# A selective-scan layer with routed experts: round-off, carries and residual move to other engines, the first chunk's front gets five PSUM banks, and the orders are planned anew

## The reference, cut to what matters

```python
x = x + mamba(layernorm(x))          # then
x = x + moe(layernorm(x))

# mamba(x):
xn = layernorm(x) * ln_g + ln_b
u, z = split(xn @ W_in.T)            # 512 + 512 features
u = silu(causal_conv4(u) + conv_b)
dt, B, C = split(u @ W_xp.T, [16, 32])
dt = softplus(dt @ W_dt.T + b_dt)    # 512 features
h = exp(dt * A) * h + (dt * u) * B   # per token, 512 features x 16 states
y = (h * C).sum(states) + u * D
return x + (y * silu(z)) @ W_out.T

# moe(x): the best 2 of 8 experts per token, weights by softmax of their logits
return sum_k w_k * (silu(x @ gate[e_k]) * (x @ up[e_k])) @ down[e_k]
```

## Time and profile before

| | us |
|---|---|
| median of 3 runs | 2536.23 (2534.64 to 2537.91) |
| profiled execution | 2529.41 |
| its span, first to last instruction | 2527.6 |
| first scan, end of the last unit (from the span's start) | 111.25, 2349.4 |
| mean granted TensorE clock | 0.848 |

### The profile page before, as it was taken

How to read it: one execution, slowest core, us unless ns; L and a number is a source line. 1 busy time by engine, 2 the same in 40 slices (tenths; PEclk the granted TensorE clock), 3 DMA queues, 4 the chain that set the end, 5 groups by cost and what they waited for, 6 DMA issues and landing times.

```text
span 2527.6 us, 31861 instructions
## 1 busy us (share of the span) xinstructions
PE 1826.6 (72%) x7502; PEld 912.5 (36%) x7502; DVE 2152.9 (85%) x3108; ACT 1629.0 (64%) x2921; POOL 1901.5 (75%) x1220
## 2 busy tenths in 40 slices
PE   5566757586878778686877678687877768665775
PEld 1112313143434344342434334343434434343543
DVE  0299999999998999899999999999999999999411
ACT  3667666667677677676767676666767667754232
POOL 0478786888878797987878797878978788888333
PEclk9877868697988888797989888798978879887898
DMA  1445444465847576575847666675757656688332
GB/s 51 118 101 117 97 113 110 104 177 147 196 126 191 138 185 159 155 178 129 205 125 188 145 164 161 155 183 135 197 135 186 155 144 163 156 225 234 101 60 35
DMA packets 217976, 369.30 MB, mean 146 GB/s; under 512 B 31040, under 2 KB 86592, under 8 KB 217664
## 3 DMA queue, kind: packets, MB, share of 16 engines
q1 hardware_dynamic: 192208, 333.56, 51.5%
q0 software_dynamic: 25584, 33.71, 6.8%
HBM read 285.05 MB, written 83.01 MB: 146 GB/s over the span
## 4 chain that ended last, share of the span: by engine, by line
PE 29%; issue 23%; DVE 19%; POOL 14%; ACT 10%; DMA 4%; POOLq 0%; DVEq 0%; ACTq 0%; SPq 0%
DVE dA L1030 10%; PE ring L568 7%; POOL arena L1260 4%; DMA out<-yt,xt 4%; PE yps L654 4%; PE ring L559 3%; ACT dA L900 3%; POOL sorted_x L1294 3%; PE ring L574 3%; DVE arena L1030 3%; PE p_g L686 3%; POOL arena L1268 2%; PE p_a L666 2%; PE ring L585 2%; POOL rst L1232 2%
## 5 line engine op out<-in xcount | busy, mean ns | idle before, releaser
L1260 POOL TENSOR_TENSOR arena<-arena,b_bc 128x2048 f32<-128x2048 f32 x256 | 1023.4, 3998 | 30.9 <-PE yps L654 30.8
L900 ACT ACTIVATE dA<-arena,a_s 128x512 f32<-128x512 f32 x1024 | 673.7, 681 | 316.9 <-DVE arena L1041 220.5
L1030 DVE TENSOR_TENSOR_SCAN dA<-dA,carry,arena 128x512 f32<-128x512 f32 x384 | 477.3, 1273 | 27.3 <-ACT dA L900 27.3
L1030 DVE TENSOR_TENSOR_SCAN dA<-dA,arena 128x512 f32<-128x512 f32 x384 | 454.0, 1213 | 42.2 <-ACT dA L900 41.6
L654 PE MATMUL yps<-arena,const_s 128*32 128x512 f32 x2048 | 328.3, 717 | 220.9 <-POOL arena L1268 179.2
L1268 POOL TENSOR_TENSOR arena<-arena,c_bc 128x511 f32<-128x511 f32 (+1 forms) x256 | 323.7, 1264 | 193.2 <-DVE arena L1030 189.7
L559 PE MATMUL ring<-arena 128*128 128x512 f32 x512 | 300.4, 717 | 198.3 <-ACT sz L825 126.0
L1304 POOL DMA_INDIRECT out<-yt,xt x135 | 218.2, 1616 | 137.4 <-DMA out<-yt,xt 67.7
L1041 DVE TENSOR_TENSOR arena<-dA,c_bc 128x1024 f32<-128x1024 f32 x256 | 312.3, 1220 | 4.4
L568 PE MATMUL ring<-arena 128*128 128x512 f32 x512 | 266.4, 668 | 21.3 <-ACT xn_t L887 9.6
L1060 DVE SCALAR_TENSOR_TENSOR t_s<-t_s,arena 128x512 f32<-128x512 f32 x64 | 158.6, 2477 | 95.5 <-ACT t_s L843 95.5
(11 more groups left out here) (147 smaller groups left out, 2870.5 us busy)
## 6 DMA issues: line engine op xcount, KB each, us to landing
arena<-dt_d SPq DMA_DIRECT2D x512, 256.0 KB, 5.6
w_e<-in_w_moe SPq DMA_DIRECT2D x105, 512.0 KB, 4.6
dt_d<-arena SPq DMA_DIRECT2D x128, 256.0 KB, 2.6
w_e<-in_w_moe SPq DMA_DIRECT2D x105, 256.0 KB, 4.4
xt<-sorted_x SPq DMA_DIRECT2D x135, 129.0 KB, 5.2
b_bc<-bc_d SPq DMA_DIRECT2D x256, 64.0 KB, 2.7
c_bc<-bc_d SPq DMA_DIRECT2D x256, 64.0 KB, 2.2
xs<-in_x SPq DMA_DIRECT2D x16, 512.0 KB, 8.6
```

The lines of the kernel that those rows point to most:

```text
L900: act.activation(dA[:, j, :], rep_dt[:, c % 2, j, :], ACT.Exp, scale=a_s[:, n, j:j + 1]).then_inc(s_exp, 1)
L1030: return dve.tensor_tensor_scan(out_ap, dA[:, j, :], hs[:, u % 3, j, :], init, ALU.mult, ALU.add)
L1260: pool.tensor_tensor(hs[:, u % 3], rep_dtu[:, c % 2], b_bc[:, g, :].unsqueeze(1).to_broadcast([P, J, T]), ALU.mult).then_inc(s_dbu, 1)
```

## The change

- **Round-off to GpSimd.** ScalarE makes t = 1 - (1 + e) in one more Identity; GpSimd adds e (`round_off`); `less_lost` now adds.
- **Carries to ScalarE.** `keep01` and `keep2` copy the last columns, each after VectorE's product; the next unit's exponentials wait for the copy.
- **Residual to TensorE.** `out_proj` adds the identity times `xs` in PSUM; ScalarE evicts the sum to `xs` (kind O in `take`). All items of the ring are now evicted by ScalarE.
- **Five banks.** The first 16 items of chunk 0 (X, U, W, P, Z, D0) go in turn to `ring` and the four banks of `dA`, before the scans need these; chunk 0 has tables of its own (`MAKES0`, `TAKES0`). The diagonal matrices of the convolution are made in four parts, VectorE's `tables` come later, and chunk 1's statistics come before all else in the front.
- **Orders.** Tables, places in the loop bodies and tile slots are new: a scatter per slot for 8 slots in place of two for 4, the last batch's tiles at +19 for +17.

```diff
-TILE_AT = [18, 20, 22, 24, 26, 28, 29, 31]
-TAIL_AT = 17
+TILE_AT = [17, 20, 22, 24, 26, 28, 29, 31]
+TAIL_AT = 19
...
-        a_slot = 2 if q >= NQ - 2 else 2
+        a_slot = 2 if q >= NQ - 2 else 1
...
-            self.at = [self.ready + k for k in [20, 21, 22, 23, 24, 25, 27, 28]]
+            self.at = [self.ready + k for k in [18, 20, 21, 22, 23, 25, 26, 28]]
...
-         (17, 0): ["O0"], (18, 0): ["O1"], (19, 3): ["F0"], (20, 1): ["F1"], (21, 4): ["R0"], (23, 4): ["K0"]}
...
+MAKES0 = {(-20, 1): ["X0", "X1"], (-19, 1): ["U0", "U1"], (-18, 1): ["W0", "U2"], (-17, 1): ["W1", "U3"], (-16, 1):
...
+FIVE = sum(q == 0 and name[0] in "XUWPZ" or name == "D0" and q == 0 for q, name in RING)
+BANK = {item: k % 5 if k < FIVE else 0 for k, item in enumerate(RING)}
+BEFORE = {}
+for k, item in enumerate(RING):
+    BEFORE[item] = next((o for o in reversed(RING[max(0, k - 5):k]) if BANK[o] == BANK[item]), None)
...
+        def bank(q, name):
+            k = BANK[q, name]
+            return dA[:, k - 1, :] if k > 0 else ring[:, :]
...
             def out_proj(q, a):
                 pe.wait_ge(s_yg, CC * (q + 1))
+                pe.wait_ge(s_xs, q + 1)
                 for i in range(2 * a, 2 * a + 2):
                     for c in range(CC):
-                        last = pe.matmul(ring[:, i % 2 * DM:i % 2 * DM + DM], sz[:, q % 2, c, i * P:(i + 1) * P],
-                                         w_out_s[:, c, :], start=c == 0, stop=c == CC - 1)
+                        pe.matmul(ring[:, i % 2 * DM:i % 2 * DM + DM], sz[:, q % 2, c, i * P:(i + 1) * P],
+                                  w_out_s[:, c, :], start=c == 0, stop=False)
+                    last = pe.matmul(ring[:, i % 2 * DM:i % 2 * DM + DM], ident, xs[:, q % 3, i, :], start=False, stop=True)
...
             def make(item):
-                k = MADE[item] - 2
-                if k >= 0:
-                    pe.wait_ge(s_ract if evictor(RING[k]) == "act" else s_rdve, TAKEN[RING[k]])
+                last = BEFORE[item]
+                if last:
+                    pe.wait_ge(s_ract, TAKEN[last])
...
             for s in range(FIRST, TOTAL_SLOTS):
+                for item in made_in(s, 0):
+                    make(item)
                 if 0 < s <= UN * NQ:
                     weigh(s - 1)
-                for item in made_in(s, 0):
-                    make(item)
...
-                act.activation(t_s[:], dtub[:, c % 2, :], ACT.Identity, bias=1.0).then_inc(s_s, 1)
+                act.activation(t_s[:], dtub[:, c % 2, :], ACT.Identity, bias=1.0).then_inc(s_one, 1)
+                act.wait_ge(s_one, v + 1)
+                act.activation(t_s[:], t_s[:], ACT.Identity, bias=1.0, scale=-1.0).then_inc(s_s, 1)
...
+                if kind == "O":
+                    act.activation(xs[:, q % 3, 2 * c:2 * c + 2, :], ring[:, :].rearrange("p (i d) -> p i d", d=DM), ACT.Copy).then_inc(s_ract, 1)
...
                 wait(act, s_m01 if j < 2 else s_m2 if j == 2 else s_h3, u)
+                if u > 0 and (u - 1) // UN % 2 == 0 and j != 3:
+                    act.wait_ge(s_carry01 if j < 2 else s_carry2, UN * ((u - 1) // UN // 2) + (u - 1) % UN + 1)
                 act.activation(dA[:, j, :], rep_dt[:, c % 2, j, :], ACT.Exp, scale=a_s[:, n, j:j + 1]).then_inc(s_exp, 1)
+            def keep01(u):
+                act.wait_ge(s_m01, u + 1)
+                act.activation(carry[:, u % UN, 0:2], dA[:, 0:2, T - 1], ACT.Copy).then_inc(s_carry01, 1)
...
-                if q % 2 == 0:
-                    dve.tensor_copy(carry[:, n, 0:2], dA[:, 0:2, T - 1]).then_inc(s_carry, 1)
...
-            def round_off(q, c):
-                dve.wait_ge(s_s, CC * q + c + 1)
-                dve.scalar_tensor_tensor(t_s[:], t_s[:], 1.0, dtub[:, c % 2, :], ALU.subtract, ALU.subtract).then_inc(s_t, 1)
...
-                dve.tensor_tensor(dst, ring[:, :].rearrange("p (i d) -> p i d", d=DM), dst, ALU.add).then_inc(s_rdve, 1)
...
+            def round_off(q, c):
+                pool.wait_ge(s_s, CC * q + c + 1)
+                pool.tensor_tensor(t_s[:], t_s[:], dtub[:, c % 2, :], ALU.add).then_inc(s_t, 1)
...
-                for c, at in enumerate((-8, -3, 0, 4)):
-                    if (s - at) % UN == 0 and 0 <= (s - at) // UN < NQ:
-                        less_lost((s - at) // UN, c)
+                for p, k in pieces(s, (-8, -2, 0, 3), (-11, -1, 1, 3)):
+                    less_lost(p, k)
...
+                for p, k in pieces(s, (-9, -3, -1, 2), (-12, -3, 0, 2)):
+                    round_off(p, k)
```

More of the change, by code:

```diff
@@ L298, in mamba_moe @@
         s_s = sem("s_s")
+        s_one = sem("s_one")
         s_l = sem("s_l")
@@ L506, in _ @@
                 front = 0 <= q + 1 < NQ
+                for g, k in tiles_in(s + 1):
+                    load_tile(g, k)
+                if q >= 0 and front and n == 9 or s == -13:
+                    store_bc(q + 1)
+                for g, k in tiles_in(s - 1, False):
+                    load_down(g, k)
                 if n == 4 and 0 <= q - 1 < NQ:
@@ L966, in _ @@
                         second_weight(p)
+                for item in taken_in(s, 0):
+                    take(item)
+                for p in ahead(s, 12, -9):
+                    norm_x(p)
                 if 0 <= s + 1 < UN * NQ:
@@ L1195, in _ @@
                     unit_second(s)
+                if n == 7 and tail:
+                    route(q - 1)
+                if unit:
+                    unit_last(s)
+                if tail and n == 2:
+                    moments(1, q - 1)
+                for p in ahead(s, 10, -21):
+                    moments(0, p)
                 if unit and n in (4, 8, 12):
```

206 lines of the change are left out of this document (97 added, 109 removed), and 24 rows, old and new, of tables (MAKES, MAKES0, TAKES, TAKES0).

## The result

The changed kernel takes 2393.45 us in the median of 4 runs (2382.61 to 2405.61) against 2536.72 us: ratio 0.9437, 95% interval 0.9391 to 0.9484, some 143 us less. The forecast was 2354 us, range 2280 to 2430. The profiled execution took 2390.97 us, its span is 2389.1.

The account below looks back on a forecast made before the run. VectorE was taken to bound the unit window (2110.94 of 2238.15 us). Front 95 + window 2075 (work 1923 + idle 152) + tail 175 = 2345 us of span, 2354 us against the median of runs; range 2280 to 2430.

Parts of the forecast that it names:

- Front, 95: Stretch before the first scan: first scan at 95 us, 16 us gained, within bounds of 6 and 25.
- VectorE's work, 2111 - 188 = 1923: Unit window: round-off 152, carries 18 and residual 18 us leave VectorE, so its work falls to 1923 us.
- reordering inside a slot adds nothing: Slots of the unit window: moving gated product, statistics and routing behind the last product adds nothing to VectorE's work.
- All of it on the engine that sets the window.: Unit window: all 188 us come off VectorE, whose work has hardly a gap that could swallow them.
- Idle, 127 + 25 = 152: VectorE's idle time in the unit window: new waits, chiefly late drive products, add 1.6 us a chunk, 25 us.
- as long as nobody waits for that item: Output projection on TensorE: the residual's extra matmuls, 30 us in all, are free on that condition.
- rival 2: Unit window: the replan removes waits, VectorE's idle halves to 64 us, time 2266 us; chance 0.13.
- Carries: Copies moved to ScalarE: 18 us off VectorE, the delay to exponentials covered; cost 0, upper end 51 us.
- Tail, 175: Stretch after the last scan: one addition earlier gives -4.6 us, two output projections cost +1.9, so 175 us.
- Rival 1: Unit window: GpSimd and TensorE become the bound, the full 100 us of new idle, 2429 us; chance 0.17.
- Rival 4: TensorE's unit reduction behind ring items in six of 16 slots delays scans; 2594 us at 2.5 us a slot; chance 0.04.
- Rival 3: VectorE beside GpSimd: other instructions wait for GpSimd's longer queue, returning 115 us, time 2469 us; chance 0.05.

Follow-up runs that it names:

- the square: Four kernels with and without the change's two halves: neither 2532 us, three moves only 2527.49, new order and five banks only 2410.98, both 2393.45.
- the moves alone: Kernel before with round-off to GpSimd, carries to ScalarE and residual to TensorE, in the old order and old front: 2527.49 us, ratio 0.9979.
- the order and banks alone: Changed kernel's tables, places and five banks, with round-off, residual and carry copies on VectorE again: 2410.98 us, ratio 0.9535.
- the one-bank run: Changed kernel with the first chunk's items all in one bank, new tables kept: 2423.07 us, ratio 0.9563.

## Why the prediction was right, and where it was not

The time came out 39 us above the forecast and inside its range; the totals of the stretches were near. That is in good part luck. The sum credits the moves with 188 us and the order within the slots with nothing, while in the square the moves alone bring 5 us and the order and banks alone 118; the errors cancelled. The signs named for being right (the first scan, VectorE's work and idle time, GpSimd 88% busy) all came near, and none of them could tell the two apart.

- **Front, 95.** Measured 87.2. The banks were credited 6 us (seven gaps of 0.84 us) and the order the rest; the one-bank run shows all but 2 us depend on the banks. In the two traces the four U items and the four convolutions take TensorE from 17.87 to 50.5 us with one bank and from 16.29 to 39.1 with five, so by the projection P the difference is 11 us (54.6 and 43.2). The other 11 arise behind it, where ScalarE waits 9.2 us for the Z items with one bank and not at all with five. The prediction counted the gaps before TensorE's items, not the waits of ScalarE behind them.
- **VectorE's work, 2111 - 188 = 1923.** Measured 1949. The 188 us were read rightly as what the three groups cost: 168 went in the old order. But "reordering inside a slot adds nothing" failed in both directions. The new order alone takes 65 us off VectorE, 60 of them from the round-off's stretch, which the sum had booked to its move. And it adds some back: before the change an independent instruction stood between a scan and its product in many places, which now follow each other directly. From the records, scan to product is 1.24 us start to start and scan to an independent instruction 1.115; some 138 more pairs are adjacent, 17 us. Putting `activate` between gave 11 us of work back and no time.
- **"All of it on the engine that sets the window."** This is the step that failed. VectorE's 94% of the window in the earlier trace rows was taken for the bound of every slot. The moves in the old order took 168 us off it and won 3 us of window. Under the new order 96 us off won 20.
- **Idle, 127 + 25 = 152.** Measured 178; the size was near, the source not as told. The drive's lateness was foreseen and costed at 25 us; it measures 57.6. The wait of the statistics for the evicted output projection was missed: TensorE's extra matmuls were called free "as long as nobody waits for that item", and the statistics did, 37.6 us in the window (the residual's own wait for TensorE, 38.0 with the order alone, went). That the replan takes idle time away (25 us) stood only in rival 2.
- **Carries.** "VectorE has 3 us before it needs those exponentials, and that covers it": alone they cost 21 us instead of gaining 18; the round-off got longer (13) and so did the wait for the exponentials (18).
- **Tail, 175.** Measured 174.5; the order alone has 175.0. The split (-4.6, +1.9) was not tested.
- **Rival 1** (GpSimd as bound, 2429) was partly at work: 21 of 55 us taken off GpSimd came out of the window. **Rival 2** had the replan's sign right. **Rival 4** (TensorE late with `weigh`) did not reach VectorE: the gated product waits 5.9 us for it, 32.4 before. GpSimd's drive does wait longer for TensorE, 63.7 us for 30.8, but with the order alone that wait is 72.1 us, and the scans wait only 5.5 us for the drive there.
- **Rival 3** (the stretch changes owner) came true in the small. No 128x512 instruction and no scan got longer; but routing's small ones, which have two operands in SBUF, now stand beside GpSimd's product. After, and before:

```profile
L1131 DVE TENSOR_TENSOR gap<-mx 128x4 f32<-128x4 f32 x16 | 14.3, 894 | 0.6
...
L1135 DVE TENSOR_TENSOR hot<-ix,const_s 128x64 f32<-128x64 uint32 x16 | 11.6, 724 | 0.6
```

```profile
L1090 DVE TENSOR_TENSOR hot<-ix,const_s 128x64 f32<-128x64 uint32 x16 | 3.6, 225 | 0.6
L1086 DVE TENSOR_TENSOR gap<-mx 128x4 f32<-128x4 f32 x16 | 2.7, 166 | 0.6
```

 That is 20 us, and a conversion (`tb` from `tbf`, 22.9 to 2.9 us) gave the same 20 back. The Trainium skill, "Perfetto Trace Analysis" (Optimizing Scalar/DVE Operations), warns that moving work between the two engines may not help. This case does not bear that out for the round-off: moved alone it took 135 us off VectorE and 52 off the time. It helped by less than its size, and 71 of the 84 us of new idle time are waits for ScalarE's exponentials.

## What to carry to other kernels

Before taking work off the busiest engine, cut the span at the period of the loop and read in each period which engine fills it: work is likely to be worth its time only in the periods where its engine is that one. An operation that stretches beside another engine's can be cured by where it stands as well as by who does it, so price a replan by the stretched rows too, and compare those rows in every run: even the residual's move, which does not touch the round-off, changed its cost by 40 us. Test a change of owner and a change of order as a square of four runs; one column of it says little (here 5 us and 118 us, together 143).
